# Phase 2 of a decoder layer with its integers transposed by DMA instead of TensorE, the down product one batch later, and the last output product moved behind gate/up of batch 0

## The reference

```python
x = layernorm(x + attention(x, w_q, w_k, w_v, w_out))      # 16 heads of 64, rotary embedding, causal softmax
x = layernorm(x + xattn(x, ctx, conv_weight))              # convolution over tokens with 3 taps; each tap is
                                                           # weighed by a cosine similarity of neighbours in ctx
x = layernorm(x + ffn(x, w_gate, w_up, w_down))            # inner size 2752

def ffn(x, w_gate, w_up, w_down):
    gate = silu(bitlinear(x, w_gate))
    up = bitlinear(x, w_up)
    return bitlinear(gate * up, w_down)

def bitlinear(x, w):                                       # activations to 8-bit integers by row, weights to -1, 0, 1
    xs = 127 / clip(max(abs(x), axis=-1), 1e-5)
    xq = clip(round(x * xs), -128, 127) / xs
    ws = clip(mean(abs(w)), 1e-5)
    wq = clip(round(w / ws), -1, 1) * ws
    return einsum('bsh,oh->bso', xq, wq)
```

## Time and profile before

| | |
|---|---|
| median of 3 runs | 1392.58 us (1391.16 to 1394.28) |
| the profiled execution, span | 1392.6 us (its own time: the span is all that the profile has of it) |
| PE busy | 1362.0 us, 98% |
| DVE busy | 1063.5 us, 76% |
| ACT busy | 622.4 us, 45% |
| POOL busy | 215.7 us, 15% |
| mean granted TensorE clock | 0.997 of full speed |
| phase 2, first gate matmul | at 834.51 us |

### The profile page before, as it was taken

One profiled execution on the slowest core, in us unless ns is written; L12 is line 12 of the kernel. 1 busy time (PEld: TensorE's weight loads), 2 busy tenths in 40 slices (PEclk: granted clock), 3 DMA queues, 4 the chain that ended last, 5 costly groups with the idle time before them and its releaser, 6 DMA issues.

```text
span 1392.6 us, 23220 instructions
## 1 busy us (share of the span) xinstructions
PE 1362.0 (98%) x7562; PEld 689.2 (49%) x7562; DVE 1063.5 (76%) x1859; ACT 622.4 (45%) x1208; POOL 215.7 (15%) x257
## 2 busy tenths in 40 slices
PE   8999999999999999999999999999999999999996
PEld 3454545555554554554555544444444444444443
DVE  6998545545678868867777778888888888888884
ACT  6887466447445535544554442223222222232221
POOL 0003221211221222122132311000000000000000
PEclk9999999999999999999999999999999999999999
DMA  9516535445354453443534582222222222222200
GB/s 378 229 42 210 200 123 204 143 131 195 124 175 127 141 181 112 161 157 112 178 138 144 131 300 78 77 75 75 75 75 75 75 75 75 75 75 75 77 22 22
DMA packets 63878, 178.96 MB, mean 129 GB/s; under 512 B 15408, under 2 KB 26848, under 8 KB 63840
## 3 DMA queue, kind: packets, MB, share of 16 engines
q1 hardware_dynamic: 63840, 178.48, 39.0%
HBM read 153.02 MB, written 25.43 MB: 128 GB/s over the span
## 4 chain that ended last, share of the span: by engine, by line
PE 51%; issue 40%; POOL 3%; DVE 2%; DMA 2%; ACT 1%; SPq 0%; POOLq 0%; ACTq 0%; DVEq 0%
PE ps L533 40%; PE ps L524 4%; PE ps L603 3%; PE ps L657 2%; PE ps L635 2%; DMA ctx<-ctx 1%; POOL q L1667 1%; POOL rstd L1662 1%; ACT prob L894 1%; DVE weights L1258 1%; POOL simw L1720 0%; PE ps L563 0%; ACT weights L856 0%; DMA weights<-wqT 0%; POOL k L1649 0%
## 5 line engine op out<-in xcount | busy, mean ns | idle before, releaser
L533 PE MATMUL ps<-weights,xT 128*128 128x512 f16 x2112 | 470.8, 379 | 2.4 <-ACT v L838 0.9
L533 PEld LDWEIGHTS ps<-weights,xT 128*128 128x128 f16 x2112 | 203.8, 98 | 237.5 <-issue 7.4
L768 PE MATMUL ps<-weights 128*128 128x512 fp8e4 (+1 forms) x1536 | 300.0, 357 | 0.1
L768 PEld LDWEIGHTS ps<-weights 128*128 128x128 bf16 x1536 | 146.8, 98 | 155.2 <-issue 0.8
L533 PE MATMUL ps<-weights 128*128 128x512 f16 x768 | 170.3, 381 | 1.5 <-DVE weights L1304 1.5
L789 PE MATMUL ps<-weights 128*128 128x512 fp8e4 x704 | 158.3, 381 | 0.0
L1062 ACT ACTIVATE weights<-ps,xscale 128x512 f32<-128x512 f32 x96 | 61.7, 643 | 170.7 <-PE ps L768 170.7
L894 ACT ACTIVATE prob<-prob,negmax,undo 128x128 f32<-128x128 f32 x256 | 122.7, 482 | 8.3 <-DVE negmax L1290 8.3
L533 PEld LDWEIGHTS ps<-weights 128*128 128x128 f16 x768 | 75.3, 98 | 92.1 <-issue 1.9
L789 PEld LDWEIGHTS ps<-weights 128*128 128x128 bf16 x704 | 67.8, 98 | 76.8 <-issue 1.6
L1662 POOL TENSOR_TENSOR rstd<-rstd,expo 128x1 f32<-128x1 f32 x32 | 17.8, 557 | 522.4 <-DVE rstd L1184 489.7
(11 more groups left out here) (171 smaller groups left out, 1809.9 us busy)
## 6 DMA issues: line engine op xcount, KB each, us to landing
wch<-w_ffn SPq DMA_DIRECT2D x96, 688.0 KB, 4.3
wch<-sim_scratch SPq DMA_DIRECT2D x96, 128.0 KB
ternary_scratch<-tern SPq DMA_DIRECT2D x48, 172.0 KB, 1.9
ctx<-ctx SPq DMA_DIRECT2D x16, 512.0 KB
wo_raw<-x_scratch SPq DMA_DIRECT2D x16, 512.0 KB, 3.3
x_in<-xT_in SPq DMA_DIRECT2D x15, 512.0 KB, 6.5
weights<-x SPq DMA_DIRECT2D x15, 512.0 KB, 10.4
x_scratch<-weights SPq DMA_DIRECT2D x15, 512.0 KB, 2.9
```

The source lines that it names most:

```text
L533: ins = nc.tensor.matmul(ps[:, bank], partsT[:, a, t], weights[:, t, w, half * HALF:(half + 1) * HALF], start=(t == 0 and a + w == 0), sto ...
L768: ins = nc.tensor.matmul(ps[:, 2 * w + a, 0:n], xqT[:, t], w8m[:, t, at:at + n], start=(t == 0), stop=(t == KT - 1))
```

## The change

In phase 2 the integers of x and of h are transposed by DMAs that SP issues, no longer by PE. They are built in another way: rounded, clamped in float32 by DVE (`clamp_x`, `clamp_h`), then brought to bfloat16 by ACT (`whole_x`, `whole_h`), a whole quarter of h each. All four quarters of h are rounded on ACT. The transposed integers go to SBUF and are not copied out of PSUM.

Down of batch i-1 runs in turn i behind gate/up of batch i (`down(i - 1, AC, hT)`), so the sum and the norm of y of batch i-2 stand in turn i on DVE, and x2 is kept in two copies on POOL (`keep_x2`). The convolution of batch i+1 has two PSUM banks of its own and stands behind the third chunk of gate/up (the fourth in turn 0). Its inputs for batch i+2 are prepared between the clamps of h. `xscale` is computed in a second pair of columns and moved. In turn 0 there is no down; instead PE runs the output product of batch 15 there, and the end of the attention of batch 15 on DVE and POOL moves into turn 1 (`turn_late`). The ternary gate and up weights are loaded earlier. After turn 15 down of batch 15 runs from an SBUF tile and PSUM banks of its own. Some attention tiles get new places in SBUF (`attn`).

The diff, cut to its core:

```diff
-HT_USES = ((0, 6), (6, 12), (12, 17), (17, 22))
+HT_PIECES = ((0, 5), (5, 10), (10, 16), (16, IT))
...
 SP, last turns of phase 1
+                    for w in range(2):
+                        sp.wait_ge(pj_full[w], pj_uses(B - 1, 2 + w) + 1)
+                    load_w8(0, 0)
+                    load_w8(0, 4)
+                    load_w8(1, 0)
                     sp.wait_ge(weighed, 3)
                     load_sims(1)
...
+                    load_w8(1, 4)
+                    sp.wait_ge(conv_free, 1)
+                    load_x1(1)
+                    load_xqT(0)
+                    store_x1(b - 1, xres)
...
 SP, phase 2
+            def load_xqT(n):
+                sp.wait_ge(xq_ready, n + 1)
+                if not (isinstance(n, int) and n == 0):
+                    sp.wait_ge(pair_full[1], n * 3)
+                apart(sp)
+                sp.dma_start_transpose(xqT, xq).then_inc(xqT_loaded, 16)
+            def load_hT(n):
+                last = isinstance(n, int) and n == B - 1
+                if isinstance(n, int) and n == 0:
+                    sp.wait_ge(padded, 2)
+                elif not last:
+                    sp.wait_ge(acc_full, n)
+                for piece, ((lo, hi), quarter) in enumerate(zip(HT_PIECES, HQ_NEEDS)):
+                    sp.wait_ge(hq_ready, n * 4 + quarter)
+                    apart(sp)
+                    sp.dma_start_transpose((hT_last if last else hT)[:, lo:hi], hq[:, lo * P:hi * P]).then_inc(hT_loaded[piece], 16)
...
+                elif kind in ("first", "steady"):
+                    sp.wait_ge(weighed, i * 3 + 6)
+                    load_sims(i + 2)
+                if kind not in ("first", "late"):
+                    store_out(i - 2)
+                if kind in ("first", "late", "steady"):
+                    sp.wait_ge(conv_free, i + 2)
                     load_x1(i + 2)
+                if kind != "last":
+                    load_xqT(i + 1)
+                load_hT(i)
...
 PE, end of phase 1
-                    out_proj(b, 0, OB)
-                    xq_T(0, 0)
-                    out_proj(b, 1, OB)
...
 PE, phase 2
+            def turn2(i, kind):
+                pe.wait_ge(xqT_loaded, i * 16 + 16)
...
                 for c, (at, n) in enumerate(CHUNKS):
                     w = c % 2
+                    if not (kind == "first" and c < 2):
+                        pe.wait_ge(pair_free[w], i * 3 + c // 2)
...
+                    if c == conv_at(kind) and kind != "last":
+                        conv(i + 1, CV)
+                if kind == "first":
+                    for c in range(2):
+                        out_proj(B - 1, c, AC)
+                    return
...
+                    pe.wait_ge(acc_free, i - 1)
+                down(i - 1, AC, hT)
...
 ACT, phase 2
                     nc.scalar.activation(silu[:, w, 0:n], ps[:, 2 * w, 0:n], ACT.Silu, scale=xscale[:, 1:2]) \
                         .then_inc(silu_ready, 1)
+                    if kind != "last" and c == at_conv + 1:
+                        round_x(i + 1)
+                    if kind != "last" and c == at_conv + 2 and c + 1 < len(CHUNKS):
+                        whole_x(i + 1)
...
+                    nc.scalar.activation(hquarter(a, hq), hquarter(a), ACT.Identity, bias=magic[:, 1:2]).then_inc(hq_ready, 1)
+                round_h(0)
+                round_h(1)
+                if more:
+                    conv_high_part(i + 2, 0)
+                whole_h(0)
+                round_h(2)
+                if more:
+                    conv_high_part(i + 2, 1)
+                whole_h(1)
+                round_h(3)
+                if more:
+                    conv_high_part(i + 2, 2)
+                whole_h(2)
+                whole_h(3)
...
 DVE, phase 2
+                chunk(0)
+                h_max(0)
...
+                    turn(B - 1, "late", False, False)
+                else:
+                    y_sum(i - 2, AC, hscale[:, 2:3], x2c[:])
+                chunk(1)
+                h_max(1)
...
+                    norm_out(y[:], i * 2).then_inc(out_ready, 1)
+                chunk(2)
+                h_max(2)
...
+                for c in range(3, len(CHUNKS)):
+                    if kind != "last" and c == at_conv + 1:
+                        residual(i + 1, CV)
+                        norm_sums(x2n)
+                    chunk(c)
                     s = h_max(c)
+                    if kind != "last" and c == at_conv + 1:
+                        norm_x(norms)
+                        scale_x()
+                    if kind != "last" and c == at_conv + 2:
+                        clamp_x(i + 1)
...
+                if kind != "last":
+                    move_xscale(i + 1)
+                if more:
+                    weigh(i + 2, 0)
+                clamp_h(0)
+                if more:
+                    weigh(i + 2, 1)
+                    conv_low_part(i + 2, 0)
+                clamp_h(1)
+                if more:
+                    weigh(i + 2, 2)
+                clamp_h(2)
+                if more:
+                    conv_low_part(i + 2, 1)
+                clamp_h(3)
+                if more:
+                    conv_low_part(i + 2, 2)
...
 DVE, last turn of phase 1
                     normalise(0)
+                    norm_x(1)
+                    scale_x()
+                    move_xscale(0)
                     mask_max(1)
...
+                    clamp_x(0)
                     normalise(1)
```

More of the change, by code:

```diff
@@ L488, in turn @@
                     store_x1(b, xres)
             turns(sp, turn, alone=2)
[L492 to L496, removed]
+            def turn2(i, kind):
+                if kind == "late":
                     sp.wait_ge(weighed, i * 3 + 6)
                     load_sims(i + 2)
-                    sp.wait_ge(pair_free[0], i * 4 + 5)
-                    load_x1(i + 2)
[L501 to L508, removed]
@@ L515, in _ @@
+            turn2(0, "first")
+            turn2(1, "late")
+            with sp.Fori(2, B - 2) as i:
+                turn2(i, "steady")
+            turn2(B - 2, "tail")
+            turn2(B - 1, "last")
+            store_out(B - 2)
+            for c in range(2):
+                half = slice(c * HALF, (c + 1) * HALF)
+                sp.wait_ge(out_ready, B + c)
+                sp.dma_start(out[B - 1][:, half], y[:, half]).then_inc(out_stored, 16)
             sp.wait_ge(out_stored, 16 * (B + 1))
@@ L562, in conv, with out_proj @@
                         for c in range(2):
[L563 removed]
+                            ins = nc.tensor.matmul(ps[:, bank + c], convw_parts[:, w, kk], conv_parts[:, kk, a, c * HALF:(c + 1) * HALF],
                                                    start=(kk == 0 and a + w == 0), stop=(kk == 2 and a == 1))
[L565 to L574, removed]
+                ins.then_inc(conv_full, 1)
+            def out_proj(n, c, bank, split=None):
+                pe.wait_ge(oT_ready, n * 2 + 2)
+                product(bank + c, oT, w_parts[:, 3], c, split).then_inc(pj_full[c], 1)
             def w_total(m):
@@ L821, in _ @@
+            turn2(B - 1, "last")
+            down(B - 1, CV, hT_last)
         @block.scalar
@@ new lines, in turn2 @@
+                if more:
[10 more added lines that the diff above has]
+                    conv_low_part(i + 2, 2)
+            turn2(0, "first")
+            turn2(1, "late")
+            turn2(2, "steady")
+            with dve.Fori(3, B - 2) as i:
+                st.loop(i - 3, DVE_TURN2)
+                turn2(i, "steady")
@@ new lines, in _ @@
+            st.end_loop(B - 5, "phase 2")
+            turn2(B - 2, "tail")
+            turn2(B - 1, "last")
+            y_sum(B - 2, AC, hscale[:, 2:3], x2c[:])
+            norm_out(y[:], 2 * B - 1).then_inc(out_ready, 1)
+            dve.wait_ge(out_stored, (B - 1) * 16)
+            for c in range(2):
+                half = slice(c * HALF, (c + 1) * HALF)
+                dve.wait_ge(acc_full, B + c)
+                st.wait(st.done(nc.vector.scalar_tensor_tensor(out=y[:, half], in0=ps[:, CV + c], scalar=hscale[:, 1:2],
+                                                               in1=x2n[:, half], op0=ALU.mult, op1=ALU.add)))
+                s = st.done(nc.vector.bn_stats(stats2[:, c], y[:, half]))
```

437 lines of the change are left out of this document (229 added, 208 removed).

## The result

The changed kernel takes 1385.38 us in the median (1381.94 to 1387.58), the kernel before, timed beside it, 1393.22 (1391.16 to 1394.28): a ratio of 0.9937, 95% interval [0.9924, 0.9951]. It is faster by 0.6%, where 1.5% was forecast. Its profiled execution took 1385.42 us with a span of 1383.6. So 1.8 us lie around the span, where the forecast had counted nothing (the profiled execution of before took 1394.28 us by the same measure, 1.7 more than its span).

The account below looks back on a forecast made before the run. PE bounded before; after the change DVE and ACT would bound the turn at 33.5 us. The sum was 822.7 + 40.6 + 36.3 + 12 x 33.5 + 25.9 + 43.9 = 1371.4 us, range 1350 to 1410 (own range 1359 to 1384).

Parts of the forecast that it names:

- the loop: Phase 2's steady turn: chain through DVE and ACT between successive turns' first chunk products, 33.5 us, longer than PE's 31.96.
- their rival: Transposed x lands late, before the next gate/up; decides from 6.9 us of landing, up to 1564 us total; chance 0.28.
- (a): DVE alone, first chunk product to fifth chunk, with y's sum and normalisation, residual, x's normalisation and scale: 15.6 us.
- (b): Fifth SiLU stands on ACT behind the rounding of x, which waits for x's scale: 1.9 us.
- (c): Fifth chunk and its maximum in the turn: 1.4 us.
- (d): Clamp of x on DVE, ACT's pass to bf16, then the last, short SiLU: 2.3 us.
- (e): Short chunk, its maximum, a copy and three small steps, until h's scale is there: 1.5 us.
- (f): ACT from h's scale: four roundings, four passes to bf16, three convolution casts, next turn's first SiLU: 10.7 us.
- the fourth rival: Steady turn of 35.0 us, each of some forty hand-overs taking 0.04 us more than read; total 1390 us; chance 0.06.
- The third rival: PE's wait in each turn halves the granted clock, costing 1.3 us in 13 turns; total 1388 us; chance 0.13.
- only moved: Start of phase 2: gate/up begins 11.8 us sooner, 10.4 of it merely the 48 output matmuls shifted behind it.
- the first rival: PE still bounds the steady turn, DVE's and ACT's work taking under 31.96 us; total 1347 us; chance 0.09.

Follow-up runs that it names:

- the reordered kernel: Changed kernel with ACT's list alone reordered: fifth SiLU ahead of the rounding of x, sixth ahead of x's pass to bf16; 1352.82 us, ratio 0.9706 to the kernel before.

## Why the prediction was right in its direction and wrong in its size

Right by the runs: after the change DVE and ACT bound the turn, in the loop that was followed from first chunk to first chunk (moving two SiLUs in ACT's list, and nothing else, took the turn to 31.97); the wait stands before the third chunk; PE's own turn is 31.97; the transposing DMAs lie beside other work, and their rival decides where it was put, between 6.4 us of landing (nothing) and 9.7 (81 us slower than the changed kernel, the clock's loss included).

The sum, term by term:

| term | forecast | measured | difference |
|---|---|---|---|
| gate/up begins | 822.7 | 821.22 | -1.5 |
| turn 0, to the next first chunk product | 40.6 | 864.66 - 821.22 = 43.4 | +2.8 |
| turn 1 | 36.3 | 902.00 - 865.56 = 36.4 | +0.1 |
| twelve turns | 402.0 | 1314.43 - 902.00 = 412.4 | +10.4 |
| to PE's last gate/up | 25.9 | 26.0 | +0.1 |
| to the end of the span | 43.9 | 44.1 | +0.2 |
| around the span | 0 | 1.8 | +1.8 |

The -1.5 is no more than executions differ by: the four kernels above that share this start of phase 2 begin gate/up between 821.29 and 823.67.

*The step that failed is the loop*, "15.6 + 1.9 + 1.4 + 2.3 + 1.5 + 10.7 = 33.4, plus 0.1", from which "only 34.39 - 33.5 = 0.9 come through". It is 34.11, and 0.28 come through. The pieces by the trace are (a) 15.9, (b) 2.0, (c) 1.4, (d) 2.3, (e) 1.5, (f) 11.0. None is far off. But 0.61 of error is two thirds of the 0.9 that the sum was to give, twelve times over: 7.3 us. The 34.11 lie within the bounds that the prediction itself gave the loop, 32.5 to 34.3 (its "own range 1359 to 1384" should have ended at 1371.4 + 13 x 0.8 = 1381.8): a sum with that margin could not tell a gain of 0.9 from almost none. In (a), y's normalisation took 0.81, not the 1.50 that I had carried over from the earlier trace rows; against that DVE waits for PE at the residual (0.36) and at the fourth chunk (0.41). These two waits show that PE's third chunk and convolution, late by the wait itself, lie on the loop as well; I had followed DVE as if PE's work were always ahead. In (f) the third cast waits for DVE's difference (0.46), as forecast, and the four passes and the hand-over are a little longer. So the fourth rival, a longer loop, had two fifths of its size (0.61 of 1.5); its cause, longer hand-overs, is at most a part of it beside the two waits for PE.

*The clock* is the second part: 3.0 of the 10.4. Two of these turns, at 902.00 and 1039.78, run most or all of their third chunk at half clock and take 35.44 and 35.79 us (+1.33 and +1.68 over 34.11). The third rival had this in every turn, at 1.3 each; it came in three turns (the third is turn 1). Windows of the changed kernel:

```profile
1040.00:1041.00 1.00, 1.00 (x3) 0.30 (x2) 1.00 (x2) 0.00 (x0) 0.00 (x0) 0.50 0.99 192
...
1076.00:1077.00 1.00, 1.00 (x6) 0.49 (x5) 1.00 (x2) 0.00 (x0) 0.00 (x0) 1.00 0.87 169
```

The waits just ahead of the three are 2.71 (turn 1), 2.62 (902.00) and 1.98 us (1039.78). The turn at 1075.57 has a wait of 1.98 as well and runs on at 1.00; why the one is followed by 1.2 GHz and the other not is open. So in the twelve turns 12 x 0.28 - 3.0 = 0.4 us of gain are left: next to nothing of what was measured comes from PE's shorter steady turn.

*Turn 0* holds 1.47 us of a wait that I hadn't seen (833.21: ACT casts for 1.04 us and loads a table for 1.28 ahead of the first SiLU at 826.10, and DVE's first product waits 3.17 for it), and some 1.0 where two operations of DVE run beside POOL's copies and ACT's last cast waits for them: ACT's list from its first pass of h to the next SiLU takes 7.8 us (855.97 to 863.79), in the reordered kernel, where these two kept their usual times, 6.8 (856.04 to 862.85).

*The start.* The prediction called 10.4 of the earlier gate/up "only moved". The run with the product back shows that the move is worth some 11 us: in turn 0 the product fills time in which PE would else stand for x's integers.

What was missed for the design lies in the prediction's own pieces (b) and (d): I priced the two trips of DVE to ACT, 1.9 and 2.3, as given, and wrote against the first rival that no reordering hides "three round trips to ACT". Two of the three can be hidden by the order of ACT's list alone, and with that rival 1 is nearly reached: a span of 1350.5 us against its 1347, with three waits left in turns 0 and 1 (1.46, 1.72 and 1.00).

Of the two rules that the prediction weighed, the trace agrees with the first only roughly. The Trainium skill, "Advanced Engine Details and Errata", X-Bar Transpose (TRN2), has transposing DMAs as fast as plain ones; here it is 3.0 against 2.2 us for the same 256 KB, and nothing hangs on the difference. The Trainium skill, "VectorE: DVE Perf Modes", The three transpose paths, gives 1309 ns for one block of 128x128, and no run here moves a single block; the prediction's estimate, which added them up to 10.5 us for x's eight, is not borne out, as these land in 3.0 us.

## What to carry to other kernels

When the engine that bounds is relieved, the gain is the distance to the next loop and no more; where that distance is a few per cent of a loop of fifty operations, a sum of single durations can't tell it, so look for the waits in that loop first. Read the in-order list of a helper engine for short work whose input is long ready, standing behind an instruction that waits: moving two SiLUs ahead of two such passes gave 32.6 us by the medians, four times the change itself. Ask each new wait for its slack: a landing of 6.4 us cost nothing where 9.7 cost 81 us.

## What the runs showed of the hardware

- A transposing DMA from SBUF to SBUF of 128x1024 bf16 lands in 3.0 us, a plain one of the same bytes in 2.2, though the queue handles three times the packets (53307 against 17184). Rows of 256 bytes do not cost what larger packets do: the earlier trace rows at one price for each packet gave 10.3 us.
- A long wait costs PE twice: at 4.9 us in each turn the granted clock was 0.50 behind the wait in both turns shown, and 1.6 to 2.75 us were lost there.
- Some of DVE's operations that begin within a copy by POOL take longer. In turn 0 a clamp takes 1.35 us and a weighing 2.05, where others of their lines take 0.51 and 1.22. It is not so each time: in the steady turn above POOL copies from 1079.73 to 1080.77 and from 1080.98 to 1082.27, and y's normalisation (1080.56, 0.81) and a chunk product (1081.28, 0.74) keep their usual times. No run changes this alone. The two slow ones and the copies beside them:

```profile
856.33 1.35 DVE L1700 TENSOR_SCALAR attn<-attn 128x688 f32<-128x688 f32 x1
857.61 2.05 DVE L1303 SCALAR_TENSOR_TENSOR weights<-wo_raw,x_in 128x1024 f32<-128x1024 f32 x1
```

```profile
856.08 1.23 POOL L1815 COPY q<-weights 128x1024 f32<-128x1024 f32 x1
857.47 1.12 POOL L1821 COPY weights<-weights 128x1024 f32<-128x1024 f32 x1 [0.15 <-POOL q L1815]
```
